# Down product of the shared expert with the hidden rows as stationary operand

## What is computed

```python
def _expert(h, g, u, d):
    return jnp.einsum('...i,hi->...h', jax.nn.silu(h @ g.T) * (h @ u.T), d)
shared_out = _expert(x, sg, su, sd)
...
out = shared_out
for e in range(E_ROUTED):
    out = out + w[..., e:e + 1] * _expert(x, rg[e], ru[e], rd[e])
...
x = x + attention_a(layernorm(x)); x = x + ffn(layernorm(x))
x = x + attention_b(layernorm(x)); x = x + ffn(layernorm(x))
```

## Time and profile before

| | |
|---|---|
| median of 3 runs | 2832.37 us (2826.76 to 2845.78) |
| profiled execution, its own time | 2840.89 us |
| its span, first to last instruction | 2839.1 us |
| mean granted TensorE clock | 0.794 |
| PE busy | 2338.6 us (82%) |
| DVE busy | 1649.9 us (58%) |
| ACT busy | 1342.0 us (47%) |
| POOL busy | 867.0 us (31%) |
| bank Y products of the shared expert (L1587), 192 records | 84.3 and 47.3 us busy |
| ACT copies of their sum (L1022), 32 | 598 ns median |
| transposes of the sum (L1592), 128 | 23.3 us busy |

### The profile page before, as it was taken

One profiled execution on the slowest core, in us unless ns is written; L12 is line 12 of the kernel. 1 busy time (PEld: TensorE's weight loads), 2 busy tenths in 40 slices (PEclk: granted clock), 3 DMA queues, 4 the chain that ended last, 5 costly groups with the idle time before them and its releaser, 6 DMA issues.

```text
span 2839.1 us, 76148 instructions
## 1 busy us (share of the span) xinstructions
PE 2338.6 (82%) x26854; PEld 1574.7 (55%) x26854; DVE 1649.9 (58%) x6164; ACT 1342.0 (47%) x2861; POOL 867.0 (31%) x934
## 2 busy tenths in 40 slices
PE   7898989898898996799956768787777878689995
PEld 4565656565565664566534545555555545456663
DVE  3777777777777776455533554444554455445553
ACT  4787878787777774344432221122221222144443
POOL 3111211111111112477760112111112211247776
PEclk7898989898888898899985565565656566589998
DMA  5000000000000000677750000000000000167875
GB/s 198 35 17 19 21 17 19 18 20 17 18 20 18 16 13 29 182 177 181 163 95 10 22 18 22 21 21 20 19 18 22 21 21 18 40 172 177 181 165 94
DMA packets 129156, 168.60 MB, mean 59 GB/s; under 512 B 16240, under 2 KB 101104, under 8 KB 128800
## 3 DMA queue, kind: packets, MB, share of 16 engines
q1 hardware_dynamic: 59168, 118.08, 13.3%
q0 software_dynamic: 51968, 37.26, 8.9%
q10 hardware_dynamic: 17664, 8.39, 1.3%
HBM read 107.55 MB, written 56.12 MB: 58 GB/s over the span
## 4 chain that ended last, share of the span: by engine, by line
PE 56%; issue 15%; POOL 10%; DVE 9%; DMA 4%; ACT 3%; POOLq 1%; ACTq 1%; DVEq 0%; SPq 0%
PE bank_S L1452 6%; POOL out_x L939 5%; POOL x L939 5%; PE bank_E L1461 5%; PE bank_T L1461 5%; PE bank_O L1517 4%; PE bank_O L1475 4%; PE bank_Y L1587 4%; PE bank_E L1535 3%; PE bank_E L1433 3%; PE bank_E L1424 3%; PE bank_E L1536 2%; DMA out_x<-yo,xs 2%; PE bank_E L1537 2%; PE bank_S L1499 2%
## 5 line engine op out<-in xcount | busy, mean ns | idle before, releaser
L980 ACT ACTIVATE z<-z,nm 128x256 f32<-128x256 f32 x1024 | 441.0, 500 | 114.8 <-DVE nm L1203 113.9
L1203 DVE CUSTOM_DVE_ANT_0 z<-bank_S,big 128x256 f32<-128x256 f32 x1024 | 380.7, 421 | 185.5 <-PE bank_S L1452 132.7
L875 POOL DMA_INDIRECT sent<-rows,slots x256 | 249.8, 976 | 248.8 <-DVE slots L1279 173.9
L1356 DVE SCALAR_TENSOR_TENSOR both<-both,bank_E 128x512 f32<-128x512 f32 (+1 forms) x228 | 155.6, 682 | 236.0 <-ACT both L1036 235.9
L939 POOL DMA_INDIRECT x<-yo,xs x152 | 237.1, 1560 | 121.9 <-DMA x<-yo,xs 43.3
L939 POOL DMA_INDIRECT out_x<-yo,xs x152 | 236.1, 1553 | 122.4 <-issue 48.7
L1452 PE MATMUL bank_S<-kx,qx 32*128 32x256 f32 x1024 | 212.5, 370 | 73.9 <-issue 32.9
L860 POOL COPY seen<-seen 128x8 f32<-128x8 f32 x32 | 6.1, 192 | 750.0 <-DVE picked L1170 714.2
L1452 PEld LDWEIGHTS bank_S<-kx,qx 32*128 32x128 f32 x1024 | 129.7, 213 | 160.1 <-issue 91.7
L1535 PE MATMUL bank_E<-xbh,w_gu 128*128 128x512 f32 (+1 forms) x342 | 178.4, 522 | 38.7 <-DMA w_gu<-w_split 25.5
L1517 PE MATMUL bank_O<-vx,probT 32*32 32x9 f32 x8192 | 120.9, 190 | 96.7 <-DVE probT L1237 85.1
(11 more groups left out here) (188 smaller groups left out, 5068.0 us busy)
## 6 DMA issues: line engine op xcount, KB each, us to landing
w_gu<-w_split SPq DMA_DIRECT2D x76, 704.0 KB, 5.4
xs<-sent SPq DMA_DIRECT2D x76, 264.0 KB, 2.8
w_dn<-w_split SPq DMA_DIRECT2D x76, 192.0 KB, 5.3
w_split<-w_gu SPq DMA_DIRECT2D x7, 704.0 KB, 3.1
both<-in_w_raw SPq DMA_DIRECT2D x8, 544.0 KB, 4.7
xin<-in_x SPq DMA_DIRECT2D x16, 256.0 KB, 2.9
sent<-rows,slots POOLq DMA_INDIRECT x256
x<-xo ACTq DMA_DIRECT2D x16, 256.0 KB, 2.3
```

The costliest lines, as they stand in the source:

```text
L875: pool.indirect_dma_start(out=sent, out_offset=bass.IndirectOffsetOnAxis(ap=slots[:, n:n + 1], axis=0), in_=rows[:, k, t, :], in_offset=No ...
L980: last = act.activation(zt, zt, ACT.Exp, bias=nm[:, n % NM_RING, t:t + 1], scale=-1.0)
L1203: last = dve.tensor_tensor_reduce(z[:, n % Z_RING, t * SEQ:(t + 1) * SEQ], bank[s][:, t * SEQ:(t + 1) * SEQ], bias_a[:, h, P - P * t:P - P ...
L1356: dve.scalar_tensor_tensor(out=a, in0=a, scalar=1.0, in1=in_blocks(q)[0:m, :], op0=ALU.add, op1=ALU.mult).then_inc(ba_ready, 1)
```

## The change

The down product of the shared expert in the passes swaps its operands: for each of the three inner tiles four products of 128 columns hold 128 tokens of hid stationary and stream here_dn, so that bank Y receives tokens by model rows at once. The step `sum` (the ACT copy) and the four transposes of `end` on PE go. The last of the twelve products signals filled Y, which DVE's `end` waits for. The semaphore down_done is counted for the first two tiles only, so the DVE waits for hid's buffers are written anew. In WORK the entry of down goes from 0.9 to 1.05, and sum and the PE part of end are removed; the scheduler therefore writes other orders for the passes. The blocks of routed experts keep their own code.

```diff
--- before.py
+++ after.py
@@ -156,7 +156,7 @@
     "logits": {"pe": 1.6, "dve": 0.3}, "route": {"dve": 0.6, "act": 0.1}, "twin": {"pool": 1.2},
     "tally": {"pool": 1.6}, "rank": {"pe": 0.7, "dve": 0.8}, "place": {"pool": 10.0},
     "gate": {"pe": 0.7, "act": 0.5, "dve": 0.6}, "up": {"pe": 0.7, "dve": 0.6},
-    "down": {"pe": 0.9}, "sum": {"act": 0.5}, "end": {"pe": 0.5, "dve": 0.6, "act": 0.1},
+    "down": {"pe": 1.05}, "end": {"dve": 0.6, "act": 0.1},
 }
 FLOW = ("pe", "act", "dve", "pool", "sync")
 
@@ -255,12 +255,8 @@
         return [("pe", "up", n), ("dve", "gate", n)]
     if step == "down":
         return [("dve", "up", n)] + ([] if n else [("dve", "rank", 0)])
-    if step == "sum":
-        return [("pe", "down", FT - 1)]
     if step == "end":
-        if eng == "pe":
-            return [("act", "sum", 0)]
-        return [("pe", "end", 0)] if eng == "dve" else [("dve", "end", 0)]
+        return [("pe", "down", FT - 1)] if eng == "dve" else [("dve", "end", 0)]
 
 def needs_before(kind, eng, step, n):
 
@@ -320,7 +316,7 @@
     out += [("route", n) for n in range(ROUTE_PARTS)] + [("twin", 0), ("tally", 0), ("rank", 0), ("place", 0)]
     for i in range(FT):
         out += [("gate", i), ("up", i), ("down", i)]
-    return out + [("sum", 0), ("end", 0)]
+    return out + [("end", 0)]
 
 def takes_part(kind, eng, step, n):
 
@@ -631,7 +627,6 @@
     gate_done, up_done = sem("gate_done"), sem("up_done")
     th_ready, a_ready, h_ready = sem("th_ready"), sem("a_ready"), sem("h_ready")
     down_done = sem("down_done")
-    summed = sem("summed")
 
     PASS_SCORES = {"A": UNITS, "B": TOK}
 
@@ -949,7 +944,7 @@
 
         @block.scalar
         def _(act):
-            for s in (exp_done, th_ready, e2_ready, summed, bxh_ready, bth_ready, bsummed, by_ready):
+            for s in (exp_done, th_ready, e2_ready, bxh_ready, bth_ready, bsummed, by_ready):
                 act.sem_inc(s, CREDIT)
 
             def attention(p, step, n):
@@ -1015,11 +1010,6 @@
                     act.wait_ge(h_ready, p.count(same(FT), n + 1 - H_RING))
                     act.activation(th[0:m, n, :], product_bank(2 * n)[0:m, :], ACT.Tanh, scale=0.5
                                    ).then_inc(th_ready, 1)
-                elif step == "sum":
-                    act.wait_ge(down_done, p.count(same(FT), FT))
-
-                    act.wait_ge(filled["Y"], use(p, "Y", -1))
-                    act.activation(total[:, :], bank["Y"][:, :], ACT.Copy).then_inc(summed, 1)
 
             def blocks(kind):
 
@@ -1298,7 +1288,10 @@
                     dve.wait_ge(a_ready, p.count(same(FT), n + 1))
                     dve.wait_ge(up_done, p.count(same(FT), n + 1))
 
-                    dve.wait_ge(down_done, p.count(same(FT), n + 1 - H_RING))
+                    if n < FT - 1:
+                        dve.wait_ge(down_done, p.count(same(FT - 1), n + 1 - (FT - 1)))
+                    else:
+                        dve.wait_ge(filled["Y"], use(p, "Y", -1))
                     dve.tensor_tensor(hid[0:m, n, :], th[0:m, n, :], product_bank(2 * n + 1)[0:m, :], ALU.mult
                                       ).then_inc(h_ready, 1)
                 elif step == "end":
@@ -1584,13 +1577,11 @@
 
                         pe.wait_ge(emptied["Y"], use(p, "Y", 2))
                     m = high(n)
-                    pe.matmul(bank["Y"][:, :], here_dn[0:m, n * P:(n + 1) * P], hid[0:m, n, :], start=(n == 0),
-                              stop=(n == FT - 1)).then_inc(down_done, 1)
-                elif step == "end":
-                    pe.wait_ge(summed, p.count(same(1), 1))
                     for t in range(TOK):
-                        last = pe.transpose(bank["Y"][:, t * P:(t + 1) * P], total[:, t * P:(t + 1) * P], ident)
-                    last.then_inc(filled["Y"], 1)
+                        a = slice(t * P, (t + 1) * P)
+                        last = pe.matmul(bank["Y"][:, a], hid[0:m, n, a], here_dn[0:m, n * P:(n + 1) * P],
+                                         start=(n == 0 and t == 0), stop=(n == FT - 1 and t == TOK - 1))
+                    last.then_inc(down_done if n < FT - 1 else filled["Y"], 1)
 
             def blocks(kind):
                 end = Pass(kind, PASSES - 1)
```

## The result

The changed kernel takes 2945.75 us (median of 4 runs, 2944.96 to 2952.31), the kernel before 2832.85 beside it: a ratio of 1.0397, 95% interval 1.0358 to 1.0436. The change makes the kernel 4% slower; the forecast was 2829, no change. The profiled execution spans 2943.5 us, 104.4 more than before. (The first turn2 of stage A starts at 111 us in the kernel before and the last at 1107, so its passes reach somewhat further than the "about 1060" given above.)

The account below looks back on a forecast made before the run. PE's stream and its waits were taken to bound the kernel, with ACT 95% full late in stage A. +36 (A) - 36 (B) - 3 (ends) = -3 us gave 2838 profiled, 2829 us as median; range 2795 to 2872.

Parts of the forecast that it names:

- Short products at v's price: Down products: four short ones cost 0.99 us like v, against 0.95 for a long one at full clock.
- Rival 4: Down products: short ones bound by weight loads, 1.49 us for 0.95, +52 us, about 2881; chance 0.05.
- The tail of B: End of a stage B pass: transposes -1.05, three downs -0.5, bturn's exposed ACT copy +0.75; -0.8 us a pass.
- Stage A +36: Stage A's 14 loop passes: the new order costs +2.6 us each, +36 us in all.
- the first half's wait at the gates: Stage A, first half: gate 1 waits behind DVE; priced at nothing, about 1 us a pass (+14) without cover.
- the two bounds: Stage A's loss a pass: PE alone, spreads ahead of the last context, +1.4 us; nearly full ACT, +1.9 to +3.1.
- Stage B -36: Stage B's 14 loop passes: -2.6 us each, -36 us in all, bounds -1.2 to -3.5 a pass.
- Its idle falls from 5.59 to some 3.7: Stage B, PE's idle before the first bmix, in us a pass, as bmix starts 1.9 us earlier.
- PE does the same work ahead of it as before: Stage B ahead of bmix: PE's work unchanged, so bmix's 1.9 us earlier start comes out of idle time.
- the short full-clock spells may fall elsewhere: Stage B: clock allowance that turned -2.7 us a pass into -2.6.
- The ends, -3: The two passes with experts alone: copy and transposes leave the path, -1.4 us each, -3 us.
- rival 2: Stage A loses more: ACT falls behind, PE longer at half clock; A +67, B -28, about 2868; chance 0.16.

Follow-up runs that it names:

- e7: The kernel before, with 28 tiny unread products run once on TensorE between stages A and B; ratio 1.0082 of before.
- e6: The change's short products with all engines' lists in the order of before, the same kernel as e1; 2871.00 us, ratio 1.0108 of before.
- e15: e9 with the first half of stage A's loop passes in the order of before on PE, ACT and DVE; ratio 1.0108 of before.
- e16: e9 with the second half of stage A's loop passes in the order of before on PE, ACT and DVE; ratio 1.0008 of before.
- e11: e9 with stage A's passes in the order of before on every engine, stage B in the change's order; ratio 0.9974 of before.
- e9: The changed kernel with 20 tiny products run once on TensorE between the stages, moving stage B's code by 80 entries; ratio 1.0078 of before.
- e5: The changed kernel measured again, unaltered; 2939.67 us, ratio 1.0349 of before.
- e10: The long products, copy and transposes of before, in the change's order on every engine in the loop passes; ratio 1.0160 of before.
- e12: e9 with TensorE's last four steps in stage A's loop passes reordered to mix 7, spread 6, context 7, spread 7; ratio 1.0163 of before.
- e8: e6 with 20 tiny products run once between the stages, moving stage B's code by 80 entries; ratio 1.0018 of before.
- e13: The kernel before with TensorE's 14 loop passes written out, other engines keeping their loops; ratio 0.9921 of before.
- e17: e11 with stage A's passes written out on TensorE only and 6 tiny products ahead of stage B's loop; ratio 0.9973 of before.
- e18: e17 with stage A's passes written out on all engines; 2805.24 us, ratio 0.9861 of before.
- e1: The change's short products in the order of before, on a chip where the kernel before takes 3107 us; ratio 1.0214.

## Why the prediction was wrong

- **Short products at v's price: right.** The rows of the line and the timeline in A (rows of the changed kernel):

```profile
L1582 PEld LDWEIGHTS bank_Y<-here_dn,both x768: 186/192/333, 141.8 to 2573.6; 128*128 128x128 f32 x128, 96*128 96x128 f32 x64
L1582 PE MATMUL bank_Y<-here_dn,both x768: 273/275/581, 141.9 to 2573.7; 128*128 128x128 f32 x128, 96*128 96x128 f32 x64
```
```profile
632.92 1.06 PE L1582 MATMUL bank_Y<-here_dn,both 128*128 128x128 f32 x8
633.81 0.60 PE L1454 MATMUL bank_E<-cst,z 128*128 128x128 f32 x4
634.25 1.95 PE L1582 MATMUL bank_Y<-here_dn,both 128*128 128x128 f32 x16
636.13 1.07 PE L1468 MATMUL bank_O<-probT,vx 128*32 128x256 f32 x16
```

  One down is 0.89 and two are 1.88 us, against 0.95 for a long one. Rival 4 is refuted: the weight loads lie under the products. The Trainium skill ("TensorE: Matmul & The Clock Gate", Back-to-back issue gap) has 81 ns for 128 columns and 131 ns for 512, a ratio of 2.5 for eight records against two; the trace does not agree, with 0.89 us against 0.95. The tail of B was put at -0.8 a pass, -11 in 14; at equal place and order (e7 and e6) B measures -10.8. That agreement is luck: the forecast was 22 us less PE work and 10.5 more waiting, and the runs have PE busy 32.5 us less (clock 0.62 for 0.60) and idle 21.9 more.
- **Stage A +36: the mechanism held, the size was low.** The two pairs shown take 138.2 and 141.6 us (138 said), turn2 starts 5.97 us after the last context's start (590.88 and 596.85) with 5.10 of PE idle, and the first half's wait at the gates, priced at nothing with a doubt of +14, is 20.1 us long in all and costs nothing (e15, e16). The loss is 45.6; the order makes 29 of it by e11 and e9, 37 by e6 and e5, 43 by before and e10. Of the two bounds, ACT's is the one that e12 and ACT's timeline support, not PE's gap, though e12's longer busy time leaves it short of a proof. In the old order the short products add 7 to 14 us to A (e6, e8, e11), and in the new one 0 to 3 (e10 against e9, e5 and the change), so the two costs don't simply add up. The 7 to 14 us stand in passes of 67.5 to 67.8 us in place of 64.8, one in before, two to five there, and A's mean clock is 0.88, 0.87 and 0.87. PE's idle time is 111 us in all three, 6 to 7 more than before. Why these passes are more is open.
- **Stage B -36: wrong, the step that failed.** "Its idle falls from 5.59 to some 3.7", said of PE before bmix, came true (3.50). What failed is "PE does the same work ahead of it as before": the same work, but from another place in the instruction stream and at another clock. "Issue" waits in B rose from 51 to 115 us, and moving the changed kernel by 80 entries takes 73 us off B (e9). The prediction read "issue" 15% in the earlier trace rows, priced nothing for it and asked nowhere what it was. The row of 1929.64 in the trace of before already showed it. The second failed term is the clock: "the short full-clock spells may fall elsewhere" was priced at 0.1 us a pass, and at the old place the new order has PE busy 41.7 us longer in 15 passes (e10), 2.8 each, with its wait ahead of bmix down by the 27 us forecast. Why the clock falls is open. At place 199 the change's B is 880.2 against 887.7, so -7.5 us; the -30.6 us before bmix are mostly given back there. PE's waits grow for ACT's `big` (+9.0; forecast as 0.75 a pass, and it is 0.76) and `kx` (+5.3) and for DVE's `xo` (+3.1), its stops at the scores of bank S by 4.9, and its busy time by 3.2 where -22 was forecast, at a mean clock of 0.59 for 0.60.
- **The ends, -3: not shown.** The stretches outside the passes are 7 us shorter, 4.8 of them ahead of the first turn2. But in e7, which has the ends of the kernel before, they are 6 us shorter than in its trace too.
- **The rivals.** Stage A lies between the forecast (+36) and rival 2 (+67), nearer to the first. No rival had stage B slower. A range that ended at 2872 took every unknown from the work and the waits, none from where the code lies.

## What to carry to other kernels

Where a TensorE stream holds long runs of very small products, read the counts between stops that nobody releases: if they repeat at 256 entries, the cost of a pass hangs on the offset of its loop in the program, and any edit ahead of it, however cheap, can be worth 40 to 70 us here. So compare two versions at equal offsets, or try a few offsets of each, before a gain or a loss is put down to the edit itself, and split the difference into busy and idle time beside the granted clock. And a stop that lies in another engine's gap (TensorE's branch in A, e13, or the gap at norm2, e12) gave next to nothing when it was removed; ask what ends last behind it.

## What the runs showed of the hardware

- TensorE's instructions come in packets of 16.4 KB, and its stops lie 256 entries apart; at 32x32 products a block is used up in 2.1 us and the next comes 3.5 to 3.8 us after the one before. After a branch back to the start of a loop PE stands 2.8 to 3.7 us (before and the change), in both stages often with a second stop soon behind it.
- 112 entries that run once changed the 15 passes of a later loop by 37.9 us (e7), 80 entries by 73 (e9) and by 13.5 (e8).
- Stage A written out on TensorE alone took 4.4 us less than before (e13) and 12.4 less than e11 (e17); written out on all engines, 39.5 less than e11 (e18). Like code differs by up to 5 us in A (e6, e8).
- In stage B the mean granted clock lies between 0.56 (e10) and 0.62 (e6) for the same or nearly the same products, with PE busy 734 and 667 us. What sets it there was not tried.
- On one chip the kernel before took 3107 us in place of 2833 to 2849. There ACT stands up to 7.1 us, PE 6.6 and DVE 5.4 in the passes of stage A (e1). In the one around 630 us the stop ends at 634.13, and the last of POOL's eight indirect transfers at 632.45. What makes that was not tried.
